# A graph layer and an expert layer on one core: swapped operands, gating inside the graph layer, slots by one-hot products, paired nodes

## The reference

```python
def graph(feat, norm, weight, w_comp, h_bias, loop_weight, src, dst, etypes):
    w_full = einsum('rb,bdo->rdo', w_comp, weight)      # 16 relations from 8 bases
    x_rel = einsum('nd,rdo->rno', feat, w_full)
    msg = x_rel[etypes, src] * norm
    agg = segment_sum(msg, dst, num_segments=N)
    return relu(agg + h_bias + feat @ loop_weight)

def ffn(x, gate_w, gate_b, w1, b1, w2, b2, gamma, beta):   # 16 experts, 256 -> 512 -> 256
    topk_vals, topk_idx = top_k(x @ gate_w + gate_b, 2)
    topk_w = softmax(topk_vals)
    h = relu(einsum('bsh,ehf->bsef', x, w1) + b1)
    out = einsum('bsef,efh->bseh', h, w2) + b2
    y = x + sum(topk_w * the two chosen rows of out)
    return layernorm(y) * gamma + beta

x = x + graph(layernorm(x), ...)
x = x + ffn(layernorm(x), ...)
```

## Time and profile before

| | us |
|---|---|
| median of 3 runs | 4463.26 (4462.36 to 4474.01) |
| the profiled execution | 4463.1 |
| its span in the profile | 4461.3 |
| PE busy | 2795.1 (63%) |
| PE weight load busy | 2486.4 (56%) |
| POOL busy | 1948.2 (44%) |
| DVE busy | 1629.5 (37%) |
| ACT busy | 488.9 (11%) |

### The profile page before, as it was taken

One profiled execution on the slowest core, in us unless ns is written; L12 is line 12 of the kernel. 1 busy time (PEld: TensorE's weight loads), 2 busy tenths in 40 slices (PEclk: granted clock), 3 DMA queues, 4 the chain that ended last, 5 costly groups with the idle time before them and its releaser, 6 DMA issues. The chain is left out here.

```text
span 4461.3 us, 66823 instructions
## 1 busy us (share of the span) xinstructions
PE 2795.1 (63%) x15198; PEld 2486.4 (56%) x15199; DVE 1629.5 (37%) x4933; ACT 488.9 (11%) x1277; POOL 1948.2 (44%) x2041
## 2 busy tenths in 40 slices
PE   4445566656666667666677766666766610999920
PEld 2224455556566566666666666666666510888820
DVE  6463343334343333333333323333332441111157
ACT  0100000000000000001111111111111100222222
POOL 2035555555555544444444444444341037222266
PEclk7566677777778778877788788788888555999965
DMA  4422323222322222222222222222222544222234
GB/s 123 114 72 86 94 87 90 82 86 82 89 85 80 86 76 77 70 65 68 70 69 68 61 72 60 67 62 61 60 66 54 200 154 123 63 63 63 63 114 138
DMA packets 241939, 374.85 MB, mean 84 GB/s; under 512 B 54862, under 2 KB 180887, under 8 KB 241844
## 3 DMA queue, kind: packets, MB, share of 16 engines
q0 software_dynamic: 101536, 232.26, 18.3%
q1 hardware_dynamic: 109619, 111.45, 7.7%
q10 hardware_dynamic: 30756, 30.81, 2.7%
HBM read 298.90 MB, written 78.45 MB: 85 GB/s over the span
## 5 line engine op out<-in xcount | busy, mean ns | idle before, releaser
L873 PE MATMUL psW<-S,msg 128*128 128x200 f32 x7248 | 1539.1, 368 | 595.3 <-issue 547.5
L873 PEld LDWEIGHTS psW<-S,msg 128*128 128x128 f32 x7248 | 1392.8, 212 | 733.1 <-issue 729.5
L806 POOL DMA_INDIRECT rows<-feat,idx x1568 | 1507.9, 962 | 538.2 <-issue 450.8
L822 DVE SCALAR_TENSOR_TENSOR S<-node,dstT,coefT 128x200 f32 x1812 | 770.2, 425 | 1959.0 <-remote 804.9
L850 PE MATMUL psG<-z,wb 128*128 (+1 forms) x3200 | 486.3, 310 | 206.2 <-issue 204.7
L850 PEld LDWEIGHTS psG<-z,wb 128*128 128x128 f32 x3200 | 460.8, 227 | 225.3 <-issue 225.2
L827 DVE COPY msg<-rows 128x256 f32 x1812 | 555.8, 307 | 63.9 <-issue 54.0
L803 POOL COPY idx<-srcT 128x14 int32 (+1 forms) x112 | 29.6, 265 | 1075.8 <-DVE msg L827 1026.1
L903 ACT COPY z<-psW 128x400 f32 (+1 forms) x250 | 123.1, 492 | 2927.9 <-PE psW L873 1831.9
L1302 POOL COPY w1x<-w1s 128x1024 f32 x116 | 120.8, 1042 | 362.9 <-PE psH L1352 356.4
L844 PE MATMUL psG<-fts,lw 128*128 (+1 forms) x400 | 82.6, 369 | 255.2 <-ACT agg L890 200.6
(11 more groups left out here) (232 smaller groups left out, 1191.5 us busy)
## 6 DMA issues: line engine op xcount, KB each, us to landing
rows<-feat,idx POOLq DMA_INDIRECT x1568
xs<-disp SPq DMA_DIRECT2D x118, 128.0 KB, 2.0
disp<-zero SPq DMA_DIRECT2D x29, 512.0 KB
eout<-os SPq DMA_DIRECT2D x114, 128.0 KB, 1.7
w1s<-in_L_ffn_w SPq DMA_DIRECT2D x2, 4096.0 KB, 21.1
w2s<-in_L_ffn_w ACTq DMA_DIRECT2D x4, 2048.0 KB
xt<-in_x SPq DMA_DIRECT2D x5, 1250.0 KB
feat<-yt SPq DMA_DIRECT2D x50, 125.0 KB
```

The lines of the kernel that those rows point to most:

```text
L806: e.indirect_dma_start(rows[:, u * H:(u + 1) * H], None, d.feat, bass.IndirectOffsetOnAxis(ap=idx[:, u:u + 1], axis=0)).then_inc(s_row[u], 16)
L822: e.scalar_tensor_tensor(S[u][:, :].rearrange("p (b n) -> p b n", n=WIN), node[:, bass.ds(nodes, WIN)].unsqueeze(1).to_broadcast([P, B, WIN]),
L873: last = e.matmul(psW[:, bass.ds(bank + c * ZC, ZC)], msg[u][:, c * P:(c + 1) * P], S[u][:, :], start=False, stop=True, skip_group_check=True)
```

## The change

**Swapped graph layer.** A window is 16 nodes, so `S` is 128 edges by 8 x 16 = 128 columns and becomes the weight matrix; the gathered rows are streamed, 256 columns, straight from the ring. A step is one matmul (two records), there is no `msg`, and the result has nodes in its rows. There are 392 windows, at most 1960 steps in 280 turns of 7, and 4 PSUM banks for open windows. POOL now waits for PE's steps before it refills half a ring, and copies the indices before the last three gathers of the half ahead. DVE builds `S` for seven steps at once by three tensor_tensor instructions; for that the coefficients are laid out step by step in the preparation (`expand`, 48 indirect gathers in 16 groups).

**Control words.** PE still reads 24 words per turn, in two halves of 12, behind the second and the sixth step of the turn before, into the other of two register sets.

**Tiles and gating inside.** A tile is 16 windows, 256 nodes, 25 tiles. Its product transposes the sums (32 transposes, four at a time, each group copied out by ACT), then multiplies by the loop matrix and the bases with the nodes in rows: 4 and 32 matmuls. DVE (`nodes`) adds bias and residual, normalises with its own reciprocal root (three rounds of multiplications) and writes `h` and `y`; PE computes the logits of the tile before. The stage of the gates is gone but for the choice itself.

**Slots by one-hot products.** For each place in the experts' slots the node that stands there is found by 100 products of one-hot matrices (114 columns each). So no rows are dispatched: the experts' stage fetches its 128 rows from `y_rows` by an indirect DMA of POOL and scatters the results by another to the nodes' two places. The copy of a slot's weights is DVE's, and `b2` is added by DVE as PSUM is read.

**Paired nodes.** Node rows are held two to a partition; the combine stage is 25 tiles of 256 nodes with plain loads. The loads of `x` (5 of 1250 KB before) now stand on ACT's queue ahead of the destinations'.

```diff
-WIN = 25
-TW = 5
+WIN = 16
+NW = -(-N // WIN)
+TW = 16
+GN2 = TW * WIN
+NT2 = -(-NW // TW)
...
-STEPS = RBLK + NW - 1
-U = 12
+STEPS = NBLK + NWP
+U = 7
+TURNS = STEPS // U
...
-ZR = 3
+NB = 4
+PART = [(0, 4), (4, 3)]
...
+AT_BANK, AT_SLOT = 0, U
+AT_CLEAR, AT_COME, AT_ENDED, AT_TILE = 2 * U, 2 * U + 2, 2 * U + 4, 2 * U + 6
+CTL = 24
...
+            xv = x[0:(NT2 - 1) * GN2, :].rearrange("(t p m) f -> p t (m f)", p=P, m=2)
+            for s, (t0, t1) in zip(s_x, XQ):
+                e.dma_start(xt[:, t0:t1, :], xv[:, t0:t1, :]).then_inc(s, 16)
+            e.wait_ge(s_xz, 1)
+            e.dma_start(xt[0:TAIL, NT2 - 1, :], x[(NT2 - 1) * GN2:N, :].rearrange("(p m) f -> p (m f)", m=2)).then_inc(s_x[len(XQ)], 16)
...
+            for g in range(SG):
+                if g >= GR:
+                    e.wait_ge(s_tp, g - GR + 1)
+                    e.wait_ge(s_tb, g - GR + 1)
+                for to, of in ((typ, d.e_typ), (dst, d.e_dst), (wgt, d.e_wgt)):
+                    e.indirect_dma_start(to[g % GR][:, :], None, of.rearrange("(j n) -> j n", n=P), bass.IndirectOffsetOnAxis(ap=jcol[:, g:g + 1], axis=0)).then_inc(s_got[g % GR], 16)
...
+            def list_in(i, q):
+                ch.add(e.tensor_copy(idx[:, q * GB:(q + 1) * GB], srcT[:, bass.ds(i * RB + q * GB, GB)]))
...
+                for q in range(2):
+                    if later(i):
+
+                        e.wait_ge(s_P, e.snap(regs[q], min_val=1, max_val=STEPS))
+                    ch.wait()
+                    e.sem_inc(s_turn, 1)
+                    for u in range(q * GB, (q + 1) * GB):
+                        if u % GB == GB - 3 and (q == 0 or not isinstance(i, int) or i < last):
+                            if later(i) or q:
+
+                                e.wait_ge(s_in, i * RB + q * GB)
+                            list_in(i + q, 1 - q)
+                        e.indirect_dma_start(rows[:, u * H:(u + 1) * H], None, d.feat, bass.IndirectOffsetOnAxis(ap=idx[:, u:u + 1], axis=0)).then_inc(s_row[u // QB], 16)
...
+            def nodes(tile1, Q):
...
+                e.wait_ge(s_tile, tile1)
+                e.wait_ge(s_st, 32 * tile1)
+                ch(e.tensor_tensor(y[0:Q, :, :], psG[0:Q, :].rearrange("p (m f) -> p m f", m=2), hb[0:Q, :].unsqueeze(1).to_broadcast([Q, 2, H]), ALU.add))
...
+                for _ in range(3):
+                    ch(e.tensor_tensor(t, v, r, ALU.mult))
+                    ch(e.tensor_tensor(t, t, r, ALU.mult))
+                    ch(e.tensor_scalar(t, t, -0.5, 1.5, ALU.mult, ALU.add))
+                    ch(e.tensor_tensor(r, t, r, ALU.mult))
...
+            def look(i):
+                e.load(regs, pairs[0:1, bass.ds(i, 1), :])
+                tile1 = e.snap(regs[1], min_val=1, max_val=NT2)
+                with e.If(e.snap(regs[0], min_val=0, max_val=1)):
+                    nodes(tile1, P)
+
+            def pair(i):
+                for h in range(2):
+                    g = 2 * i + h
+                    if later(i):
+                        e.wait_ge(s_S, g - 1)
+                    s0 = g * U
+                    e.tensor_tensor(hot[h][:, :, :], dstS[:, bass.ds(s0, U)].unsqueeze(2).to_broadcast([P, U, WIN]),
+                                    node[:, :].unsqueeze(1).to_broadcast([P, U, WIN]), ALU.is_equal).then_inc(s_hot, 1)
+                for h in range(2):
+                    g = 2 * i + h
+                    e.wait_ge(s_hot, g + 1)
+                    e.tensor_tensor(hot[h][:, :, :], hot[h][:, :, :], wgtS[:, bass.ds(g * U, U)].unsqueeze(2).to_broadcast([P, U, WIN]), ALU.mult).then_inc(s_scl, 1)
+                for h in range(2):
+                    g = 2 * i + h
+                    s0 = g * U
+                    e.wait_ge(s_scl, g + 1)
+                    if later(i):
+
+                        e.wait_ge(s_P, s0 - U)
+                    e.tensor_tensor(S[h][:, :].rearrange("p (s b n) -> p s b n", s=U, b=B), hot[h][:, :, :].unsqueeze(2).to_broadcast([P, U, B, WIN]),
+                                    coefS[:, bass.ds(s0 * B, U * B)].rearrange("p (s b) -> p s b", b=B).unsqueeze(3).to_broadcast([P, U, B, WIN]),
+                                    ALU.mult).then_inc(s_S, 1)
+                if later(i):
+                    look(i)
+            turns(e, TURNS // 2, pair)
+            look(TURNS // 2)
+            nodes(NT2, HALF)
+
+        @blk.tensor
+        def _(e):
+            e.sem_inc(s_zT, NC)
...
+                def z_columns(g):
+                    q, c = divmod(g, HC)
+                    e.wait_ge(s_zT, tile1 * NC + max(g - 1, 0))
+                    for k in range(4):
+                        w = 4 * q + k
+                        last = e.transpose(psT[g % 2][:, k * P:(k + 1) * P], z[:, w * H + c * P:w * H + (c + 1) * P], ident[:, :])
+                    last.then_inc(s_tp, 1)
...
+                def basis_part(m, c):
+                    for b in range(B):
+                        at = ((c * B + b) * 2 + m) * P
+                        last = e.matmul(psG[0:Q, m * H:(m + 1) * H], zT[:, at:at + Q], wb[:, c, b, :], start=False, stop=(c == HC - 1 and b == B - 1))
+                    return last
+                groups = HC * nw // 4
+                z_columns(0)
+                z_columns(1)
+                y_columns(tile1, P)
+                for g in range(2, groups):
+                    z_columns(g)
+                e.wait_ge(s_ft, tile1 * 16)
+                e.wait_ge(s_gr, tile1)
+                loop_part(0)
+                for c in range(HC):
+                    e.wait_ge(s_zT, tile1 * NC + groups - HC + 1 + c)
+                    basis_part(0, c)
+                logits(tile1, P)
+                loop_part(1)
+                basis_part(1, 0)
...
+            def turn(i, h, ahead):
+                regs, other = sets[h], sets[1 - h]
+                for k, (u0, n) in enumerate(PART):
+                    tile1 = e.snap(regs[AT_TILE + k], min_val=1, max_val=NT2)
+                    with e.If(e.snap(regs[AT_ENDED + k], min_val=0, max_val=1)):
+                        tile_product(tile1, TW)
+                    clear = e.snap(regs[AT_CLEAR + k], min_val=1, max_val=NWP)
+                    come = e.snap(regs[AT_COME + k], min_val=1, max_val=NBLK)
+                    bank = {u: e.snap(regs[AT_BANK + u], min_val=0, max_val=(NB - 1) * BANK) for u in range(u0, u0 + n)}
+                    slot = {u: e.snap(regs[AT_SLOT + u], min_val=0, max_val=(RB - 1) * H) for u in range(u0, u0 + n)}
+                    e.wait_ge(s_clear, clear)
+                    e.wait_ge(s_in, come)
+                    if k == 0:
+                        e.wait_ge(s_S, i * 2 + h + 1)
+                    for u in range(u0, u0 + n):
+                        e.matmul(psW[:, bass.ds(bank[u], H)], S[h][:, u * ZC:(u + 1) * ZC], rows[:, bass.ds(slot[u], H)],
+                                 start=False, stop=True, skip_group_check=True).then_inc(s_P, 1)
+                        if ahead and u in HALVES:
+                            c0, c1 = HALVES[u]
+                            e.load(other[c0:c1], ctl[0:1, bass.ds(i * 2 + h + 1, 1), c0:c1])
+            with e.Fori(0, TURNS // 2 - 1) as i:
+                turn(i, 0, True)
...
+            def tiles(t, nw):
...
+                for k in range(nw):
+                    if later(t) and k == nw // 2:
+                        e.wait_ge(s_tile, t)
+                        columns_in(t)
+                    e.wait_ge(s_P, e.snap(regs[k], min_val=1, max_val=STEPS))
+                    at = k % NB * BANK
+                    e.copy(z[:, k * H:(k + 1) * H], psW[:, at:at + H]).then_inc(s_z, 1)
+                    e.wait_ge(s_z, t * TW + k + 1)
+                    e.copy(psW[:, at:at + H], zero[:, :]).then_inc(s_clear, 1)
...
+                for g in range(HC * nw // 4):
+                    q, c = divmod(g, HC)
+                    if g == 2:
+                        y_out(t, P)
+                    e.wait_ge(s_tp, t * NC + g + 1)
+                    e.copy(zT[:, c * B * GN2:(c + 1) * B * GN2].rearrange("p (b w n) -> p w b n", b=2 * B, n=WIN // 2)[:, 4 * q:4 * q + 4, :, :],
+                           psT[g % 2][:, :].rearrange("p (w b n) -> p w b n", w=4, b=2 * B)).then_inc(s_zT, 1)
...
+            for j in range(NT * K):
+                t, k = divmod(j, K)
+                if j % (GT * K) == 0:
+                    g = t // GT
+                    if g >= 2:
+                        e.wait_ge(s_inv, (g - 1) * GT * K)
+                    e.tensor_tensor(in_lane[g % 2][:, :, :], lane[:, :].unsqueeze(1).to_broadcast([P, GT * K, P]),
+                                    lo[:, g * GT:(g + 1) * GT, :].rearrange("p t k -> p (t k)").unsqueeze(2).to_broadcast([P, GT * K, P]), ALU.is_equal).then_inc(s_lane, 1)
+                if j >= D:
+                    e.wait_ge(s_inv, j - D + 1)
+                e.tensor_scalar(in_tile[j % D][:, :], tile_no[:, :], hi[:, t, k:k + 1], row[:, t, k:k + 1], ALU.is_equal, ALU.mult).then_inc(s_tile, 1)
...
```

(51 more changed lines are left out.)

1616 lines of the change are left out of this document (806 added, 810 removed).

## The result

The kernel after takes 3918.45 us (median of 4 runs, 3904.31 to 3943.87) against 4462.93 for the kernel before beside it: a ratio of 0.878 (95% interval 0.873 to 0.883). The forecast was 3500 us with a range of 3150 to 3850: the direction holds, but a little over half of the gain came (544 us of 963).

The account below looks back on a forecast made before the run. PE was taken as the bound (2095 busy, 792 starved, 201 behind ACT of the graph layer's 3153 us). Preparation 250, graph layer 2497 and the rest 750 made 3497, with 1.8 outside the span 3500 us; range 3150 to 3850.

Parts of the forecast that it names:

- starvation after: Graph layer: PE's lost time beside gathers follows instructions fetched or issued, falling from 7.1 to 2.8 us per group.
- Rival B: Graph layer: starvation stays whole, 7.1 us for each of 112 groups whatever PE runs; 3855 us in all, chance 0.13.
- the larger of PE and POOL counts: Graph layer tiles: POOL 1.3 us a block sets the first three (712 us), PE the other 22 (1750 us).
- the steps' records: Graph layer: each step's matmul records and sequencer work take 0.60 us on PE, 1176 us for 1960 steps.
- a product with its waits for ACT: Graph layer, end of each tile: transposes, matmuls and logits take 28 us on PE, bounds 25 and 36.
- DVE's `S`: Graph layer: PE stalls 6 us per tile because DVE's `nodes` stands ahead of the next `S`, bounds 0 and 9.
- rival A: Graph layer: no starvation, 2321 us, or 2219 with a stall of 0 too; 3220 to 3320 in all, chance 0.25.
- Preparation: Stage before the graph layer: from 283 to about 250 us, bounds 210 and 300.
- choice and slots: Stage replacing gates and dispatch: choice 43 us, one-hot products 100 x 0.45, ends 17; 105 us, bounds 80 and 140.
- experts: Experts stage: 480 us against 487, with POOL's two indirect DMAs a slot (3.0 us) hidden under 4.27.
- combine: Last stage: plain loads in place of 100 gathers take 155 us against 193, bounds 105 and 193.
- Rivals C and D: Graph layer: C, control-word reads bound PE, 4080 us, chance 0.03; D, sequencer's control flow is dear, 4740 us, chance 0.02.

Follow-up runs that it names:

- the plain-load kernel: Kernel after with each of the 1568 indirect gathers replaced by a plain load of 128 whole rows: 2841.8 us.
- the kernel with one clear: Kernel after with POOL clearing one column of its own tile behind each gather, without waiting: 3317.22 us without the stall, 3955.89 with it.

## Why the prediction was wrong, point by point

**The step that failed** is "starvation after": that PE's stall beside the gathers follows the number of instructions which PE and DVE run per step, so that 7.1 us a group become 2.8. Measured are 7.4 (829.6 / 112) by the label, and 6.1 without what ends at a signal of rows. PE's instructions per step fell to less than half and the stall hardly moved; a quarter of the bytes didn't move it; only POOL's gathers, their kind and their pace, did. Rival B, with the stall whole, said 3855 us and is the case that came, 63 us under the median. I gave it 0.13 and ended the range on it.

**What B still lacked** is the second error of the same step: that in the first tiles the larger of PE and POOL counts. The first three tiles took 893 us (268 to 1161) where 712 were forecast: PE's steps wait 345 us for issue (79 of it ends at a signal of rows), and POOL waits 150 us for blocks that a stalled PE has not freed. The other 22 took 2044 (1161 to 3205) where 1785 were forecast. There issue idle time is 459 us, 65 of it at a signal of rows, against 203 for starvation: that alone is 191 to 256 of the 259 us.

**The other terms** came out near their forecast. In those 22 tiles the steps' records take 846 us (816 forecast), a product with its waits for ACT some 30 (28), and PE waits 82 us for DVE's `S` (129). The timeline of PE in the plain-load kernel, where nothing stalls, at a clock of 0.98:

```profile
1502.95 7.39 PE L1121 MATMUL psW<-rows,S 128*128 x32
...
1516.41 7.85 PE L1121 MATMUL psW<-rows,S 128*128 x26 [2.95 <-DVE S L1025]
...
1541.97 1.04 PE L1070 MATMUL psZ<-ident,z 128*128 128x128 f32 x8
...
1563.46 2.75 PE L1121 MATMUL psW<-rows,S 128*128 x12
```

Between the first row and the third lie 60 steps (120 records) in 36 us (1541.97 less 1502.95 less 2.95 behind DVE), 0.60 each, as taken; over the whole layer it is 0.61 (1075.2 busy and 125.4 idle for issue, 1960 steps). The product takes 21.5 us (1541.97 to 1563.46), against 24.5 at full clock and under the bounds of 25 and 36. PE waits 53 us for DVE's `S`, 2.1 a tile, against 6, inside its bounds.

**Without the stall the sum comes out, by luck.** With no starvation it gave 2321 us for the graph layer and 3323 for the whole (rival A). On a chip without the stall the kernel with one clear took 2335 and 3317. But two errors cancel. With the product at 21.5 us and the wait for `S` at 2.1, the same sum gives 2155 us; the 180 missing are the frame's, which took the larger of 1.3 us a block and PE's time for the whole: PE waits 429 us for rows there, because either engine pays for the other's pauses.

**Preparation** was 268 against 250, **choice and slots** 99 against 105, **experts** 491 against 480, **combine** 147 against 155. In the experts POOL's two transfers fit under the slot as forecast; PE waits 39.6 us for fetched rows (59 times, 1.7 us at most), which I had at nothing. Rivals C and D fall: a read of 12 words takes 851 ns where nothing stalls, and the 560 branches there leave at most 125 us of idle time together with all other issue.

**What the change is worth** thus depends on the chip. The stall costs the kernel before 1030 to 1090 us (4463 to 4518 against 3430) and the kernel after some 600 to 660 (3918 to 3975 against 3317, where it ran with one clear, not unchanged). With the stall the ratio is 0.88, without it 0.967. Of some 520 us between the two profiled executions, 289 are behind the graph layer, 216 in it and 15 in the preparation. Without the stall (one clear in both) the graph layer loses 206 us and the rest gains 328; with the 152 us of the gates' work set beside the old layer, it is 54 lost and 176 gained. So the swapped layer pays because the stall takes less from it (2937 against 2335, 602 us) than from the old one (3153 against 2129, 1024 us). What in the change eats up its gain where nothing stalls, no run separates; PE's wait of 429 us for rows stands there where the old layer waits 273 us for `msg`. With plain loads in both, on two chips, the ratio is 2841.8 / 3037.76 = 0.935: there neither the stall nor POOL's gathers are in the way, and most of the gain is again outside the graph layer.

## What to carry to other kernels

An engine idle for "issue" while another engine works is a coupling to be measured before it is sized: I had its 792 us in the rows, but scaled them by a cause that I had only guessed. One run with the suspected work in a cheaper form (plain loads in place of indirect ones) names the cause in numbers. "Issue" is a remainder: it also takes in waits whose ending event the trace has lost. Check it against the durations of the sequencer's own instructions, which hardly vary where nothing stalls (55 to 65 ns at PE's steps). Compare two kernels stage by stage as well as whole: the gain of the tail hid a graph layer that gains nothing where nothing stalls. Where two engines meet over a ring, a stall of the one is paid by both in turn, so the larger of the two times is a lower bound and no estimate.

## What the runs showed that I had not expected

The same program takes 4463 to 4518 us on some chips and 3430 on two others. On the first, instructions of PE's and DVE's sequencers last up to 1.4 us while POOL writes indirect gathers 1.25 us apart. In the kernel before (where nothing stalls, the trace is that with one clear) the difference lies in the graph layer, 3153 against 2129 us, and is more than the idle time itself: issue idle time is 792 against 7 us, and PE's busy time 2095 against 1798, at clocks of 0.74 and 0.80 in the two halves against 0.95. Why those two are free of it no run here tells. With the stall, 0.1 us more between gathers took the kernel after from 0.88 of before to 0.807 (3625 us, one run), at a price of 102 us where there is no stall. No version here is the best on both.
